# A selective-scan state loop: channel halves side by side in an SBUF ring, B and C loaded together, seven drives on GpSimd

## The reference, cut to what matters

```python
x_proj, z = jnp.split(x @ W_in + b_in, 2, axis=-1)
u = _silu(x_proj)
A = -jnp.exp(A_log)
Bm, Cm = jnp.split(u @ W_x + b_x, 2, axis=-1)
dt = jax.nn.softplus(u @ W_dt + b_dt)
def step(h, inp):
    u_t, dt_t, B_t, C_t = inp
    dA = jnp.exp(dt_t[..., None] * A)
    h = h * dA + (dt_t * u_t)[..., None] * B_t[:, None, :]
    y_t = jnp.einsum('bds,bs->bd', h, C_t) + D_param * u_t
    return (h, y_t)
...
y = y * _silu(z)
return y @ W_out + b_out
```

## Time and profile before

| | us |
|---|---|
| median of the runs | 362.44 |
| profiled execution | 363.72 |
| its span | 361.6 |
| TensorE busy | 312.2 |
| VectorE busy | 298.3 |
| ScalarE busy | 214.9 |
| GpSimd busy | 188.1 |

### The profile page before, as it was taken

How to read it: one execution, slowest core, us unless ns; L and a number is a source line. 1 busy time by engine, 2 the same in 40 slices (tenths; PEclk the granted TensorE clock), 3 DMA queues, 4 the chain that set the end, 5 groups by cost and what they waited for, 6 DMA issues and landing times. The chain is left out here.

```text
span 361.6 us, 5633 instructions
## 1 busy us (share of the span) xinstructions
PE 312.2 (86%) x1750; PEld 236.5 (65%) x1750; DVE 298.3 (82%) x743; ACT 214.9 (59%) x504; POOL 188.1 (52%) x225
## 2 busy tenths in 40 slices
PE   8858396798998998699777989897899989999993
PEld 5646395696665747444446855575698658989873
DVE  0899999997988898999999999999949334844945
ACT  4666323233255867579488548797556566765742
POOL 2499997664514053878768797968404600100111
PEclk9989689999999999899989999999999999999998
DMA  8920000000000004454443435344100000000011
GB/s 227 418 100 2 1 0 3 0 1 2 0 2 1 0 4 147 122 158 153 140 137 128 162 106 171 129 132 133 58 2 0 2 0 1 3 0 2 1 31 29
DMA packets 11668, 24.44 MB, mean 68 GB/s; under 512 B 1247, under 2 KB 2399, under 8 KB 11383
## 3 DMA queue, kind: packets, MB, share of 16 engines
q1 hardware_dynamic: 11639, 24.09, 20.0%
HBM read 23.50 MB, written 0.59 MB: 67 GB/s over the span
## 5 line engine op out<-in xcount | busy, mean ns | idle before, releaser
L1070 POOL TENSOR_TENSOR arena<-arena 128x512 f32<-128x512 f32 x63 | 81.0, 1289 | 34.0 <-DVE arena L741 30.4
L741 DVE TENSOR_TENSOR_SCAN arena<-arena,ps 128x512 f32<-128x512 f32 x64 | 77.3, 1209 | 0.1
L1341 ACT ACTIVATE arena<-arena,neg_a 128x508 f32<-128x508 f32 x64 | 43.4, 714 | 6.9 <-DVE arena L741 6.8
L734 DVE TENSOR_TENSOR ps<-arena,ps 128x512 f32<-128x512 f32 x64 | 43.3, 678 | 1.9 <-PE ps L1787 1.9
L769 DVE TENSOR_REDUCE arena<-ps 128x2 f32<-128x496 f32 x32 | 21.4, 667 | 24.8 <-PE ps L1849 24.8
L1803 PE MATMUL ps<-first_in,arena 128*128 128x128 f32 x256 | 40.0, 280 | 1.2 <-POOL arena L1070 1.1
L1115 POOL TENSOR_TENSOR rstd<-veps,mhalf 128x4 f32<-128x4 f32 (+2 forms) x6 | 5.0, 838 | 67.5 <-DVE veps L843 35.5
L1803 PEld LDWEIGHTS ps<-first_in,arena 128*128 128x128 f32 x256 | 32.7, 145 | 10.5 <-issue 3.3
L1787 PE MATMUL ps<-arena,pick_wide 96*128 96x512 bf16 x64 | 25.1, 397 | 15.6 <-DVE arena L741 14.8
L1618 PE MATMUL ps<-arena,first_in 128*128 128x128 f32 (+1 forms) x192 | 25.7, 295 | 10.6 <-POOL arena L966 10.6
L1618 PEld LDWEIGHTS ps<-arena,first_in 128*128 128x128 f32 x192 | 24.7, 209 | 13.0 <-POOL arena L966 12.8
(11 more groups left out here) (287 smaller groups left out, 768.5 us busy)
## 6 DMA issues: line engine op xcount, KB each, us to landing
arena<-c_rows_dram SPq DMA_DIRECT2D x64, 256.0 KB, 3.2
fold_in<-in_fold_dram SPq DMA_DIRECT2D x1, 2056.0 KB, 11.0
late_in<-in_late_dram SPq DMA_DIRECT2D x1, 1423.5 KB, 16.9
early_in<-in_early_dram SPq DMA_DIRECT2D x1, 921.5 KB, 12.8
xres<-in_x_dram SPq DMA_DIRECT2D x1, 512.0 KB, 13.6
kv_ctx<-in_context_dram SPq DMA_DIRECT2D x1, 480.0 KB, 6.8
rows_in<-in_rows_dram SPq DMA_DIRECT2D x1, 384.0 KB, 14.1
first_in<-in_first_dram SPq DMA_DIRECT2D x1, 320.0 KB, 5.1
```

Of the source, the lines that this page charges most:

```text
L734: tt(chain(q), dtu[:, n, cols(g)], chain(q), ALU.mult).then_inc(S("drive"), 1)
L741: nc.vector.tensor_tensor_scan(hist[:, q % NBUF], fade[:, q % NFADE], chain(q), 0.0, ALU.mult, ALU.add).then_inc(S("scan"), 1)
L1070: tt(seen[:, q % NBUF], hist[:, q % NBUF], c_wide[:, q % NBUF], ALU.mult).then_inc(S("read_out"), 1)
L1341: act(fade[:, q % NFADE].rearrange("p (b t) -> p b t", t=T)[:, :, 1:], dt[:, n, cols(g)].rearrange("p (b t) -> p b t", t=T)[:, :, 1:], ACT ...
```

## The change: what it does

The loop goes by states d = 0 to 31 (group, then state). From state 4 on both channel halves are one item of 1024 columns (`ITEMS`); states 0 to 3 stay in halves, first all four for half 0, then for half 1. Drive, history and read-out share one slot of a ring of five in SBUF: the drive is written into the slot, the scan runs in place, the read-out multiplies in place, and TensorE reads it from there (eight transposes). B comes by DMA with C: the rows are stored in the order B0, C0, B1, C1, ... (`by_state` in the weights), and one load of two rows fills `bc_wide`, four buffers. For states 0 and 1 B comes from TensorE (a float32 matmul into banks 1 and 2), and the load brings C only. The drives of states 7, 11, 15, 20, 23, 26 and 29 are made by GpSimd, each after the read-out three states earlier. The bf16 splitting, the selector and the widening matmuls are gone. The decay has four buffers for both halves in place of six. PSUM banks freed by this let y have four banks of its own; the turning back and gating of y for group 0 come later in the loop, and those for group 1 after it. The second softplus comes ahead of the loop in the list of ScalarE, with its table loads.

```diff
             for g in range(2):
                 sp.wait_ge(S("xdbl"), g + 1)
-                sp.dma_start(c_rows[:, cols(g)], bc_f[NS:2 * NS, cols(g)]).then_inc(S(f"c_stored{g}"), 16)
-                for q in range(g * NK4, (g + 1) * NK4):
-                    sp.wait_ge(S(f"c_stored{g}"), 16)
-                    if q >= NBUF:
-                        sp.wait_ge(S("read_out"), q - NBUF + 1)
-                    sp.dma_start(c_wide[:, q % NBUF], c_rows[q % NS, cols(g)].partition_broadcast(P)).then_inc(S(f"c_wide{q % NBUF}"), 16)
+                sp.dma_start(bc_rows[g], bc_f[0:2 * NS, cols(g)]).then_inc(S(f"bc_stored{g}"), 16)
+                for d in range(g * NS, (g + 1) * NS):
+                    s = d % NS
+                    sp.wait_ge(S(f"bc_stored{g}"), 16)
+                    if d >= NWIDE:
+                        sp.wait_ge(S("read_out"), through(d - NWIDE))
+                    if d < 2:
+                        sp.dma_start(wide(d, 1), bc_rows[g, 2 * s + 1].partition_broadcast(P)).then_inc(S(f"bc_wide{d % NWIDE}"), 16)
+                    else:
+                        sp.dma_start(bc_wide[:, d % NWIDE], bc_rows[g, 2 * s:2 * s + 2].partition_broadcast(P)).then_inc(S(f"bc_wide{d % NWIDE}"), 16)
...
+        ITEMS = [(d, n, n + 1) for n in range(NH) for d in range(LEAD)] + [(d, 0, NH) for d in range(LEAD, ND)]
+        BY_POOL = (7, 11, 15, 20, 23, 26, 29)
...
-                tt(chain(q), dtu[:, n, cols(g)], chain(q), ALU.mult).then_inc(S("drive"), 1)
...
-                nc.vector.tensor_tensor_scan(hist[:, q % NBUF], fade[:, q % NFADE], chain(q), 0.0,
+            def drive_of(i):
+                d, first, last = ITEMS[i]
+                if d in BY_POOL:
+                    return
+                at = cols(d // NS)
+                if d >= NRING:
+                    ve.wait_ge(S("seen_used"), through(d - NRING))
...
+                if d < 2:
+                    ve.wait_ge(S("b_mm"), d + 1)
+                    tt(slot(d)[:, first], dtu[:, first, at], bank(1 + d), ALU.mult).then_inc(S("drive"), 1)
+                elif last - first == 1:
+                    ve.wait_ge(*wide_ready(d))
+                    tt(slot(d)[:, first], dtu[:, first, at], wide(d, 0), ALU.mult).then_inc(S("drive"), 1)
+                else:
+                    ve.wait_ge(*wide_ready(d))
+                    tt(slot(d), dtu[:, :, at], both(wide(d, 0)), ALU.mult).then_inc(S("drive"), 1)
+
+            def scan_of(i):
...
+                state = slot(d)[:, first:last].rearrange("p h t -> p (h t)")
+                nc.vector.tensor_tensor_scan(state, fade[:, d % NFADE, first:last].rearrange("p h t -> p (h t)"), state, 0.0,
                                              ALU.mult, ALU.add).then_inc(S("scan"), 1)
...
+            drive_of(0)
+            for i in range(2 * LEAD):
+                drive_of(i + 1)
+                scan_of(i)
+                between(i)
+            for q in range(2 * LEAD, NQ, 2):
+                i = item_at(q)
+                if i + 1 < NI:
+                    drive_of(i + 1)
+                between(q)
+                scan_of(i)
+                between(q + 1)
...
+            def seen(i):
+                d, first, last = ITEMS[i]
+                po.wait_ge(S("scan"), i + 1)
+                po.wait_ge(*wide_ready(d))
+                if last - first == 1:
+                    tt(slot(d)[:, first], slot(d)[:, first], wide(d, 1), ALU.mult).then_inc(S("read_out"), 1)
+                else:
+                    tt(slot(d), slot(d), both(wide(d, 1)), ALU.mult).then_inc(S("read_out"), 1)
+
+            def drive_of(d):
+
+                po.wait_ge(*wide_ready(d))
+                po.wait_ge(S("seen_used"), through(d - NRING))
+                tt(slot(d), dtu[:, :, cols(d // NS)], both(wide(d, 0)), ALU.mult).then_inc(S("pool_drive"), 1)
...
-            for q in range(NQ - 1):
...
-                tt(seen[:, q % NBUF], hist[:, q % NBUF], c_wide[:, q % NBUF], ALU.mult).then_inc(S("read_out"), 1)
+            for q in range(NQ - 2):
+                if q < 2 * LEAD or q % 2 == 0:
+                    seen(item_at(q))
+                if q % 2 == 0 and q // 2 + 3 in BY_POOL:
+                    drive_of(q // 2 + 3)
```

More of the change, by code:

```diff
@@ L344, in query_bank, with latent_bank @@
         def query_bank(g, h):
-            return bank(7 if g == 0 and h >= 4 else 6 + h % 2)
+            return bank((6 if g else 1) + h % 2)
+        def latent_bank(g):
+            return bank(7 if g else 3)
         def within_chunk(tt, c):
@@ new lines, in scan_of @@
+            def scan_of(i):
+                d, first, last = ITEMS[i]
+                ve.wait_ge(S("fade"), i + 1 if i < 2 * LEAD else 2 * (d + 1))
+                if d in BY_POOL:
+                    ve.wait_ge(S("pool_drive"), BY_POOL.index(d) + 1)
+                else:
+                    ve.wait_ge(S("drive"), i + 1 - sum(e < d for e in BY_POOL))
+                state = slot(d)[:, first:last].rearrange("p h t -> p (h t)")
+                nc.vector.tensor_tensor_scan(state, fade[:, d % NFADE, first:last].rearrange("p h t -> p (h t)"), state, 0.0,
@@ L778, in normal5, with between @@
                 tt(pr, pr, s5_rden[:, u % 2].unsqueeze(2).to_broadcast([P, 2, KV]), ALU.mult).then_inc(S("prob5"), 1)
[L780 to L785, removed]
-                    landed(3, 1, 7)
[L787 to L792, removed]
+            def between(q):
+                if q == 3:
+                    landed(3, 1, 7)
+                if q == NK4 + 3:
                     gate_turned(0)
-                if q == NK4 + 3:
                     gate_turned(1)
@@ L804, in _ @@
                         shift(u)
[L806 to L810, removed]
+            drive_of(0)
[10 more added lines that the diff above has]
+                between(q + 1)
+            last = ND - 1
+            ve.wait_ge(S("scan"), NI)
+            tt(slot(last), slot(last), both(wide(last, 1)), ALU.mult).then_inc(S("read_last"), 1)
             def add5(b):
@@ L1352, in _ @@
             ac.wait_ge(S("neg_a"), 2)
-            fading(0)
-            fading(1)
-            fading(2)
+            for f in range(LEAD):
+                fading(f)
+            table_of(ACT.Softplus)
+            softplus(1, 6)
+            table_of(ACT.Exp)
+            for f in range(LEAD, NH * LEAD):
+                fading(f)
             def latents_out(g):
                 ac.wait_ge(S("turned"), 3 * B + HB * (g + 1))
-                act(kvT[:, g * HB:(g + 1) * HB, TC:], bank(6 + g).rearrange("p (b t) -> p b t", b=HB), ACT.Identity,
+                act(kvT[:, g * HB:(g + 1) * HB, TC:], latent_bank(g).rearrange("p (b t) -> p b t", b=HB), ACT.Identity,
                     bias=W("be_lat"), scale=W("g_lat")).then_inc(S("kvT_lat"), 1)
@@ L1424, in _ @@
                     rows_b(1, 7)
[L1425 to L1429, removed]
+                if q == NK4 + 2:
+                    y_out(0)
+                    y_out(1)
                 if q == 24:
@@ L2017, in _ @@
                         similar(u)
-            accumulate(NQ - 2)
-            accumulate(NQ - 1)
-            pe.wait_ge(S("scan"), NQ)
+            accumulate(NI - 1)
             mixed = 0
```

264 lines of the change are left out of this document (113 added, 151 removed).

## The result

The changed kernel takes 437.53 us (four runs, 435.85 to 440.2) against 362.50 for the kernel before: ratio 1.207, 95% interval 1.2011 to 1.2136. Forecast were 430 us, own range 412 to 446, and slower with a chance of 0.82. The profiled execution took 440.20 us, the longest of the four; its span is 438.4 us, 76.8 longer than before.

What follows compares the result with a forecast made beforehand. VectorE was taken to bound the loop, TensorE the rest. With turns the loop is 190 us against 123.5: +66.5 - 0.6 + 1.5 = +67.4 on 363.72 gives 431.1, less 1.3: 430 us; own range 412 to 446, wider 357 to 446.

Steps and rivals of the forecast that it cites:

- The mechanism: State loop: VectorE operations with two SBUF inputs, scan included, and GpSimd's SBUF operations take whole-operation turns, less 0.14 us.
- Rivals 1 and 2: Loop, scan leaves port free: 1, drives and GpSimd take turns, 365 us, chance 0.17; 2, VectorE sets pace, 351, 0.11.
- rival 3: Loop: GpSimd's reads slip into the scan's free clocks, half of 68 us shared; loop 156, total 396 us, chance 0.07.
- The sizes: Loop, lone durations at 1024 columns: drive 1225 ns, scan 2.28 us, GpSimd operation 2347 ns.
- The sum of turns: State loop: all turns of drives, scans, read-outs and GpSimd's other operations add up to 187 us.
- GpSimd's drives: Loop: seven drives each move a turn of 1.09 us to one of 2.21, costing 7.8 us within the 187.
- VectorE's other work in the loop lies beside GpSimd's turns: Loop: maxima, reciprocals and statistics on VectorE cost nothing extra; uncovered, up to 10 us.
- handovers of 0.05 us each: Loop: an extra cost per handover, counted only in the upper end of the own range, 446 us.
- Start-up: Start of the loop: idle while drives 2 and 3 need the first loads, between 1.3 and 5 us, 3 taken.
- Loads: Loop: 512 KB per state lands in 3.2 to 6.4 us, covered by two states of some 5.6 us; costs nothing.
- Start and tail: Before the first drive 0.6 us less; end of the loop 1.5 us more, up to 4 if TensorE runs at half rate.
- the wider one: Whole kernel: the range from 357 to 446 us, holding rival 3 and nearly all of rival 1, leaving out rival 2.

Runs made afterwards that it cites:

- e3: The kernel before, with the drive written into the history buffer and the scan run in place, so only the scan has two SBUF inputs: 399.38 us, ratio 1.1049.
- e8: The changed kernel with the transposes of a state's read-out one state later in TensorE's list, from state 18 on: 434.14 us, ratio 1.1957.
- e9: The kernel e8 with VectorE making all the drives, none on GpSimd: 427.69 us, ratio 1.1779.
- e1: The changed kernel with GpSimd's seven drives back on VectorE: 427.59 us, ratio 1.1805.
- e2: As e1, with all read-outs on VectorE too: 408.79 us, ratio 1.1286.
- e4: The kernel before, with the drive reading both inputs from SBUF and still writing PSUM; the scan keeps its PSUM operand: 379.72 us, ratio 1.0476.
- e5: The kernel before, with 12 of its 64 half-step drives made by GpSimd in SBUF and those steps' decay in PSUM: 367.04 us, ratio 1.0103.

## Why the prediction was right

- **The mechanism** was the forecast's: turn-taking by whole operations, with 0.14 us of overlap. Rivals 1 and 2 (the scan leaves the port free) fall by e3; rival 3 (half of it shared) falls by the scans' 4.43 us, which hold the whole read-out, and by the GpSimd drive's 4.33, which waits for a scan's end. The sizes held: 1.19 to 1.23 for the drive (1.225 taken), 2.28 for the scan (2.28), 2.34 for GpSimd (2.347), 5.47 a state (5.44).
- **The sum of turns**, 187 us, was 187.3. Errors in it cancelled: GpSimd's four late operations and its small ones took 7.6 us where 5 were taken, and drives and read-outs somewhat less than their price.
- **GpSimd's drives** were priced at 7.8 us; the loops of e8 and e9 differ by 7.6. In the order of the change the stop of TensorE behind them adds to it: 11.9 between the loops (200.1 and e1's 188.2), 9.9 between the whole kernels.
- **What was mis-sized: the term "VectorE's other work in the loop lies beside GpSimd's turns".** It was counted at nothing, with 10 us as the price uncovered. The turn was free for 9.8 us beyond the start-up. 5.1 of them are stretches in which pieces of the next attention in VectorE's order waited for TensorE, which stood behind a late read-out and then ran at half its clock; without that order they are gone (e8). So it was less the length of that work than what it waited for. The other uncovered price, handovers of 0.05 us each, did arise: 4.6 us over some 119 turns.
- **Start-up** idle was 3.0 us for the 3 taken (3.4 in e8), in part by luck: 1.4 of them are the first two drives, which read PSUM and stood in no term. VectorE waited 2.59 and 0.90 us for loads, partly beside GpSimd's turns.
- **Loads** landed in 3.6 us (bounds 3.2 and 6.4) and were hidden, but for the start: of 5.47 x 2 us they and the read-out need 6.
- **Start and tail** came as forecast (-0.7 and +0.95 for -0.6 and +1.5; the three terms of the 1.5 add up to 1.65). TensorE's granted clock was 0.76 on average in the loop, between the levels of 1.2 and 2.4 GHz, where it was 0.97 before, and 1.00 from 337 us on, where TensorE was busy without a break (13.00 of 13 us); so it cost the tail nothing. That it would cost time inside the loop was not in the forecast.
- The forecast was 7.5 us under the measured time, of 75; its own range and the wider one held.

## What to carry to other kernels

Before moving an operand from PSUM to SBUF, or work from VectorE to GpSimd, count which VectorE operations will have two SBUF inputs while GpSimd reads SBUF: in these traces their durations add up as if both were on one engine, and GpSimd's are the longer. Fewer instructions were then no gain here: one operand in PSUM, as the kernel before had it, was worth more than merged loads and wider operations. And a late result of one engine stops TensorE's in-order list with everything behind it, so put independent work ahead of a consumer that may be late.

## What the runs showed that was not expected

- Taking the read-outs from GpSimd as well (e2 against e1) was worth 18.8 us although VectorE then did all of drives, scans and read-outs alone.
- With a sum of turns of 1.67 in a period of 1.71, turn-taking was hidden only until the first disturbance, and cost 17.6 us (e4).
- An engine 8 us less busy gave no time back (e5): its waits grew by 7.9 us. That TensorE's in-order list behind GpSimd's longer queue is the reason fits the rows, but is not shown. No version run here beat the kernel before.
